# Another order for the burst period of an attention phase: turns of x between other work, the last batch's statistics first

## The reference, cut to what matters

```python
x = x * s1[:, None, :]
x = (x - mu) * rsqrt(var + EPS_IN)                  # statistics over the 512 features
q = heads(einsum('bsh,oh->bso', x, q_weight) * q_dc)
k = heads(einsum('bsh,oh->bso', x, k_weight) * k_dc)
v_flat = einsum('bsh,oh->bso', x, v_weight) * v_dc * s2
attn = softmax(q @ k^T * scale)                     # 16 heads of 32, 128 x 128 per batch
out = einsum(attn @ v, w_weight) * w_dc
skip = einsum(v_flat, u_weight) * u_dc
return out + skip
```

## Time and profile before

| what | us |
|---|---|
| median of 3 runs (4097.18 to 4099.27) | 4098.18 |
| the profiled execution's own time | 4101.49 |
| its span in the profile | 4099.2 |
| TensorE busy | 3759.8 |
| a period of the loop without a burst | 19.41 |
| a burst period (most of them) | 24.04 |

### The profile page before, as it was taken

One profiled execution on the slowest core, in us unless ns is written; L12 is line 12 of the kernel. 1 busy time (PEld: TensorE's weight loads), 2 busy tenths in 40 slices (PEclk: granted clock), 3 DMA queues, 4 the chain that ended last, 5 costly groups with the idle time before them and its releaser, 6 DMA issues. The chain is left out here.

```text
span 4099.2 us, 63717 instructions
## 1 busy us (share of the span) xinstructions
PE 3759.8 (92%) x22112; PEld 2314.7 (56%) x22112; DVE 3024.1 (74%) x3172; ACT 1332.9 (33%) x2013; POOL 1877.7 (46%) x1444
## 2 busy tenths in 40 slices
PE   8999669999997899999878999997999839999999
PEld 6777423334344677777666777775777613333344
DVE  4767679999995777777466777753666758999997
ACT  3555311111112433343243333432455511111111
POOL 2655635555553134443313444433455645555554
PEclk9999869999998899999979999998999969999999
DMA  3666745555553122222231222213566765656563
GB/s 121 239 245 245 280 166 180 189 180 188 181 188 123 56 70 78 79 78 65 80 100 60 77 78 76 73 63 125 185 239 241 265 230 162 189 180 193 176 192 118
DMA packets 270514, 619.95 MB, mean 151 GB/s; under 512 B 34112, under 2 KB 36928, under 8 KB 270304
## 3 DMA queue, kind: packets, MB, share of 16 engines
q1 hardware_dynamic: 265952, 608.74, 44.7%
q10 hardware_dynamic: 4352, 8.39, 0.6%
HBM read 380.58 MB, written 236.45 MB: 151 GB/s over the span
## 5 line engine op out<-in xcount | busy, mean ns | idle before, releaser
L1156 DVE CUSTOM_DVE_ANT_0 l0r_g<-l0r_g,l0r_pv,l0r_cf 128x1024 f32<-128x1024 f32 x512 | 674.3, 1339 | 68.6 <-PE l0r_pv L962 45.7
L1156 DVE CUSTOM_DVE_ANT_0 l3r_g<-l3r_g,l3r_pv,l3r_cf 128x1024 f32<-128x1024 f32 x512 | 673.9, 1339 | 67.6 <-PE l3r_pv L962 46.8
L962 PE MATMUL l3r_pv<-l3r_x,l3r_wv 32*128 32x512 f32 x1024 | 260.3, 507 | 24.4 <-POOL l3r_wv L882 16.7
L962 PE MATMUL l0r_pv<-l0r_x,l0r_wv 32*128 32x512 f32 x1024 | 261.7, 510 | 21.5 <-POOL l0r_wv L882 15.1
L974 PE MATMUL l0r_py<-l0r_g,l0r_cd 128*32 128x512 f32 x2048 | 281.1, 623 | 0.0
L962 PEld LDWEIGHTS l0r_pv<-l0r_x,l0r_wv 32*128 32x128 f32 x1024 | 97.3, 187 | 323.1 <-issue 203.3
L962 PEld LDWEIGHTS l3r_pv<-l3r_x,l3r_wv 32*128 32x128 f32 x1024 | 96.5, 186 | 323.9 <-issue 201.9
L974 PE MATMUL l3r_py<-l3r_g,l3r_cd 128*32 128x512 f32 x2048 | 278.9, 618 | 0.1
L1912 POOL TENSOR_TENSOR l2h_st<-l2h_veps,l2h_mhalf 128x1 f32<-128x1 f32 x32 | 17.6, 549 | 351.1 <-DVE l2h_veps L1800 351.1
L1912 POOL TENSOR_TENSOR l1h_st<-l1h_veps,l1h_mhalf 128x1 f32<-128x1 f32 x32 | 17.6, 549 | 350.9 <-DVE l1h_veps L1800 350.9
L102 PE MATMUL l1h_ps_p<-l1h_xh,l1c_wh 128*128 128x512 f32 x384 | 162.9, 424 | 8.8 <-DVE l1h_xl L1826 8.3
(11 more groups left out here) (455 smaller groups left out, 9896.2 us busy)
## 6 DMA issues: line engine op xcount, KB each, us to landing
l0r_x<-xhl_s SPq DMA_DIRECT2D x128, 512.0 KB, 11.4
l3r_x<-xhl_s SPq DMA_DIRECT2D x128, 512.0 KB, 11.4
xhl_s<-l0a_xo SPq DMA_DIRECT2D x116, 512.0 KB, 4.6
xhl_s<-l3a_xo SPq DMA_DIRECT2D x116, 512.0 KB, 4.6
gate_s<-l0a_gate SPq DMA_DIRECT2D x64, 256.0 KB, 2.8
l0r_dx<-dx_s SPq DMA_DIRECT2D x32, 512.0 KB, 13.3
l0r_gate<-gate_s SPq DMA_DIRECT2D x32, 512.0 KB, 13.9
l0r_crow<-feed_s SPq DMA_DIRECT2D x64, 256.0 KB
```

The costliest lines, as they stand in the source:

```text
L962: last = pe.matmul(pv[j % 2][:, h * HALF:(h + 1) * HALF], wv[r, q, 2 * t + j % 2, :], x[r, q, t, j % 2, :], start=True, stop=True)
L1156: dve._custom_dve(bass.dve_ops.TENSOR_ADD_SAT, out=g[:, t, j, :], in0=g[:, (t - 1) % TS, j, :], in1=pv[j % 2][:, :], s0=cf[:, q, t, 0, j:j ...
```

## The change

Three lists of jobs and the order of the banks are changed, for burst periods alone. TensorE's was: scores, turn 0, U, X0, X1, values 0, turn 1, W, X2, X3, values 1, turn 2, Q. It becomes: X0, scores, turn 0, X1, U, X2, values 0, turn 1, X3, W, values 1, turn 2, Q. VectorE takes the statistics first and X0's low half before `peak`, X1's after it, X2's after `scale_u`, X3's before `scale_w`. ScalarE takes X0's high half first, then `keep_pt`, X1's, the normalisation, X2's, `exponent`, `keep_pt`, X3's. No instruction is added or taken out. The burst p = -1 is one of the periods that the new lists cover; its `sum_columns(Q)` and `sum_columns(K)` stood ahead of X0 and now stand behind X1, and `sum_columns(V)` stood between X1 and X2 and now stands between X2 and X3.

```diff
-        BURST = ("U", "X0", "X1", "W", "X2", "X3", "Q", "K", "V")
+        BURST = ("X0", "X1", "U", "X2", "X3", "W", "Q", "K", "V")
...
# TensorE
+                if burst:
+                    turn_x(p, "X0")
                 scores(p)
                 turn(g, 0)
+                if burst:
+                    turn_x(p, "X1")
                 mix_u(p)
                 if p.first(-1):
                     sum_columns(Q)
                     sum_columns(K)
                 if burst:
-                    turn_x(p, "X0")
-                    turn_x(p, "X1")
+                    turn_x(p, "X2")
                 if p.first(-1):
                     sum_columns(V)
...
                 values(g, 0)
                 turn(g, 1)
+                if burst:
+                    turn_x(p, "X3")
                 mix_w(p)
-                if burst:
-                    turn_x(p, "X2")
-                    turn_x(p, "X3")
                 values(g, 1)
                 turn(g, 2)
...
# ScalarE
+                if burst:
+                    high_x(p, "X0")
                 keep_pt(g, 0)
                 if burst:
-                    high_x(p, "X0")
+                    high_x(p, "X1")
+                    normalise(p.plus(4))
+                    high_x(p, "X2")
                 exponent(p, 0)
+                keep_pt(g, 1)
                 if burst:
-                    high_x(p, "X1")
-                keep_pt(g, 1)
+                    high_x(p, "X3")
...
-                normalise(p.plus(4))
+                if not burst:
+                    normalise(p.plus(4))
                 exponent(p, 1)
-                if burst:
-                    high_x(p, "X2")
-                    high_x(p, "X3")
...
# VectorE
+                if burst:
+                    statistics(p.plus(4))
+                    low_x(p, "X0")
                 peak(p)
+                if burst:
+                    low_x(p, "X1")
                 centre(p, 0)
                 scale_u(p)
                 if burst:
-                    low_x(p, "X0")
-                    low_x(p, "X1")
-                statistics(p.plus(4))
+                    low_x(p, "X2")
+                else:
+                    statistics(p.plus(4))
...
                 centre(p, 1)
+                if burst:
+                    low_x(p, "X3")
                 scale_w(p)
-                if burst:
-                    low_x(p, "X2")
-                    low_x(p, "X3")
```

## The result

| | before | after |
|---|---|---|
| median, us (5 runs each) | 4097.55 | 4080.24 (4074.26 to 4081.36) |
| ratio, 95% interval | | 0.9954 (0.9941 to 0.9968) |
| the profiled execution's own time, us | 4101.49 | 4080.76 |
| its span, us | 4099.2 | 4078.5 |

A second measurement of the same changed kernel, among the experiments, gave 0.9942 (0.9929 to 0.9956). The medians moved by 17.3 us here and by 24.2 there (4101.37 to 4077.13), and the two intervals overlap; the forecast was 22.

A forecast was written before the change was run, and what follows sets the result against it. Bound in bursts by a ring between engines, not TensorE's own work. Profiled 4101.49 - 23.6 (bursts) - 4.7 (clock) - 7.0 (p = 3) + 13.3 (lead) = 4079.5; median 3.31 lower, 4076.2, range 4067 to 4088.

The forecast's parts named there:

- The steady burst: Each burst from p = 7 on: 24.04 us shortens to 22.05, taken as 1.97 saved; twelve bursts give 23.6.
- the forecast waits ahead of U and X3: In the steady burst, TensorE stalls 0.34 us before U for X0's low half and 0.4 before X3 for `scale_u`.
- the walk: Timing of a burst by each engine's start-to-start times; X3 waits for U's bank, takes 0.58 us, W starts at 7.9.
- The half clock: Three bursts at clock 0.93 cost 1.57 us more each; with idle time down from 2.24 to 0.75, 4.7 gained.
- p = 3: First burst of a layer, without U or W: Q starts at 9.4 against 12.92, saving 3.5 us a layer, 7.0.
- The lead: Burst p = -1: Q's sum, behind X1, waits for batch 1; all behind 6.65 us later, cost 13.3.
- rival 2: The lead: clock rises later behind the small matmuls, K and V at half clock, 2.6 us a layer, 4081.5; chance 0.07.
- 1 (dips stay): Bursts: the half-clock dips stay or come back, 4.7 us less gain, 4081; chance 0.10.
- 3 (the lead is free): The lead costs nothing, hidden by something or the sums speed up: 4063, halfway 4069; chance 0.07.
- 4 (a longer chain): VectorE's chain in the burst about 1 us longer, U and X3 wait on: 12 us less gain, 4088; chance 0.10.
- 5: Burst's early statistics wait for GpSimd's `scale_x`, with x some 8 us late: 4111.5; chance 0.06 together with 6.
- 6: Burst: new order has no effect, the 2.95 us lost are the turns' own cost: 4111; chance 0.06 together with 5.

The follow-up runs named there:

- e2_stats_late: Changed kernel, but the last batch's statistics back behind U's read-out and X2's low half, its normalisation behind the second block copy: 4140.02 us, ratio 1.0095.
- e6: Kernel before, with only the early statistics (first on VectorE in bursts) and normalisation; turns, banks and half order old: 4092.33 us, ratio 0.9980.
- e7: e5 with the statistics moved out of the burst to the end of the period before, ahead of V's read-out: 4053.56 us, ratio 0.9887.
- e5: Changed kernel, old TensorE order at p = -1; in bursts U's read-out, low halves X2, X3 earlier (VectorE), X3's high half ahead of first exponent (ScalarE): 4064.46 us.
- e4: Changed kernel, but in bursts VectorE reads out U and takes X2's low half ahead of the first centre: 4086.94 us, ratio 0.9965.
- e1: Changed kernel, but at p = -1 TensorE turns X0 and X1 behind the sums of Q and K again: 4066.19 us, ratio 0.9912.
- e3: Kernel before, with TensorE's list of p = -1 alone in the new order: 4117.34 us, ratio 1.0032.

## Why the prediction was right, and where a term was off

- **The steady burst.** 22.05 forecast, 22.03 measured, with the forecast waits ahead of U and X3. One step of the walk was right by luck: it let X3 take 0.58 because a turn is longer from a standstill. In e2_stats_late X3 stands still for 3.49 us and W still follows 0.41 behind it. The 0.59 in the changed kernel is a wait of its own, W's for X2's low half, which the forecast had in time. Shown in its parts: the two halves of the change need each other. The early statistics alone leave the burst at 24.03 (e6), the new turns alone make it 26.41 (e2), both give 22.03. That VectorE's chain sets the pace is shown best by e7, where taking the statistics out of it gave 21.5 against e5's 21.89, as worked out. e4 and e5 add that the chain's end runs over ScalarE: it moved to Q in e4, and the new order on both engines gave 21.89.
- **The half clock.** Forecast 4.7 us; none of the 24 bursts in two traces of the changed kernel has a dip (nor one of the 48 in e1, e4, e5 and e7), against six of 24 with the old burst, four of these at p = 7. The outcome is right. My reason, less idle time in all, is not: e6 has the same 2.25 us of idle time, cut up otherwise, and no dip. The rule that only longer gaps matter (Trainium skill, "TensorE: Matmul & The Clock Gate", "Why this matters for your kernels") would have left the dips; with 3.49 us the trace agrees with it in twelve of twelve bursts, but dips behind waits of 1.15 it does not explain. What decides there stays open.
- **p = 3.** Forecast 3.5 a layer. With X0 counted in, 2.8 and 3.7 in the first trace, 3.5 and 4.0 in the second. The number is right because two errors nearly cancel. Q was to start at 9.4 and starts at 10.2 to 10.9: the turns behind a wait of 2.8 to 3.2 us, X2 first, run at half clock (four turns last 1.09 us instead of 0.60), where the walk had them at full clock. And the half-clock loss behind Q, left in the forecast as it was (11.77 from Q to the next scores), is gone in three of the four (10.4) and smaller in the fourth (11.01).

```profile
1423.35 1.09 PE L1453 MATMUL l1h_ps_p<-l1h_ident,l1h_x 128*128 128x128 f32 x4 [3.18 <-DVE l1h_xl L1830]
...
1428.43 0.76 PE L102 MATMUL l1h_ps_p<-l1h_xh,l1c_wh 128*128 128x512 f32 x1
```

- **The lead.** The step was right: Q's sum waits for batch 1 (e1, e3). The size was off: 5.6 and 5.5 us to the first scores instead of 6.65 each. Q's first product came 6.6 later in layer 1 as forecast, but the clock rose sooner behind it: before, it was 0.50 for the first 5.24 us, after, 0.64 on average in the first 4.75. In layer 2 it was the other way round: 0.67 on average in the first 5.24 us before, 0.50 for the first 4.75 after. So the clock moves the first scores by up to 1 us in either direction, and rival 2, a clock that rises later behind the long sums, is not borne out. In layer 2 Q came 4.8 later and not 6.6, since batch 1's normalisation started at 22.36 within the phase instead of 24.21: ScalarE had waited 1.9 us less for K's weight. An earlier lead does not keep all that it gains: in e5_tight the first scores come 12.2 us earlier than in the changed kernel, but periods 0 to 2 take 4.8 longer (21 products at half clock in each layer instead of 11 and 16), and attention is 8.2 shorter. Rows below: the clock in layer 1 before and after, then in layer 2; ScalarE in layer 2, before and after.

```profile
1341.76:1347.00 5.24, 5.24 (x12) 4.13 (x13) 4.16 (x8) 4.18 (x5) 0.00 (x0) 0.50 0.00 0
```
```profile
1351.25:1356.00 4.75, 4.75 (x14) 3.81 (x15) 3.76 (x8) 3.69 (x5) 0.00 (x0) 0.64 0.00 0
```
```profile
2087.99:2093.23 5.24, 5.24 (x16) 4.20 (x17) 4.16 (x8) 4.19 (x5) 0.00 (x0) 0.67 0.00 2
```
```profile
2083.65:2088.40 4.75, 4.75 (x11) 3.77 (x12) 3.76 (x8) 3.69 (x5) 0.00 (x0) 0.50 0.00 2
```
```profile
2065.59 1.91 ACT L1583 ACTIVATE l2c_wh<-l2h_o 128x2048 fp32r<-128x2048 f32 x1 [5.51 <-DMA l2h_o<-L_kT]
...
2069.21 0.80 ACT L1608 ACTIVATE l2h_x<-l2h_x,l2h_st 128x512 f32<-128x512 f32 x1
```
```profile
2054.59 1.91 ACT L1585 ACTIVATE l2c_wh<-l2h_o 128x2048 fp32r<-128x2048 f32 x1 [3.59 <-DMA l2h_o<-L_kT]
...
2058.21 0.80 ACT L1610 ACTIVATE l2h_x<-l2h_x,l2h_st 128x512 f32<-128x512 f32 x1
```

- **The sum.** Attention forecast -22.0, measured -25.6: the twelve bursts brought 29.6 with their dips (forecast 28.3), p = 3 6.5 (7.0), and the leads cost 11.1 (13.3); 0.6 lies elsewhere. The total forecast 4076.2, measured 4080.2, 4.0 above. Three things make that up: attention 3.6 better, the scans 4.8 longer, and the profiled execution only 0.5 us above the median instead of 3.3. The sum carried neither of the last two, so that the total came out within 4 us is in part luck.
- **The rivals.** 1 (dips stay), 3 (the lead is free) and 4 (a longer chain) are out by the rows above, 2 by the two layers' clock. 5 did not happen: the statistics start 0.61 behind V's read-out without a wait. 6 is out, the 2.95 us were waits: 2.5 of them are gone in e7.

## What to carry to other kernels

When transposes feed a product through a small ring of buffers, walk the ring engine by engine from the start of the period, with each instruction's start-to-start time: such a walk gave a burst to 0.02 us. Look for work that is ready early and stands late in an in-order list, and for idle time of the same engine one period earlier, which is worth more than the front of the crowded period (0.4 us a burst from e5 to e7). A list that is shared by a steady state and its lead should be priced in the lead too: here 11 of 37 us were given back in one period of each layer's 44.

## What the hardware showed that I had not expected

- TensorE's granted clock stays at 0.50 (1.2 GHz) from 1326.66 to 1349.70 in the changed kernel's lead, 23.04 us in which the engine is busy without a gap with the sums' small products and the turns between them. It rises 2.7 to 6.1 us behind Q's first product in the twenty leads of the ten traces.
- The same wait of 1.15 us is followed by a half-clock stretch in three of twelve bursts and not in the others; a wait of 3.49 us is, in twelve of twelve.
- Phases with unchanged code vary by 9 us between executions, beside a change that brings 17 to 26 us.
